# Routed experts' weight scales: one bfloat16 sum an expert earlier, five weight slots, expert 0 prepared during routing, the second token tile turned by TensorE

## The reference, cut to what matters

```
logits = x @ wg.T;  gates = softmax(logits)
w_topk, idx_topk = top_k(gates, 8);  w_topk /= sum(w_topk)
buf = zeros(64, 160, 256).at[se, rank].set(x[st], mode='drop')   # tokens of each expert
h = einsum('ech,efh->ecf', buf, expert_w1)                       # 64 x (1536 x 256)
x1, x2 = split(h, 2)
out = einsum('ecf,ehf->ech', x1 * silu(x2), expert_w2)           # 64 x (256 x 768)
combined = zeros(2048, 256).at[st].add(out[se, rank] * w)        # where rank < 160
return shared_expert(x) + combined
```

## Time and profile before

| | us |
|---|---|
| median of 3 runs | 2089.8 (2089.48 to 2091.47) |
| the profiled execution, whole | 2087.55 |
| its span, first to last instruction | 2085.5 |
| TensorE busy | 2045.9 |
| VectorE busy | 1606.5 |
| ScalarE busy | 1399.0 |
| GpSimd busy | 492.7 |
| recurrence, feed-forward and dense experts | about the first 1333 |
| routing and shared expert | about 1333 to 1459 |
| routed experts | 1459 to the end |

### The profile page before, as it was taken

How to read it: one execution, slowest core, us unless ns; L and a number is a source line. 1 busy time by engine, 2 the same in 40 slices (tenths; PEclk the granted TensorE clock), 3 DMA queues, 4 the chain that set the end, 5 groups by cost and what they waited for, 6 DMA issues and landing times. The chain is left out here.

```text
span 2085.5 us, 84981 instructions
## 1 busy us (share of the span) xinstructions
PE 2045.9 (98%) x34658; PEld 1904.1 (91%) x34658; DVE 1606.5 (77%) x8214; ACT 1399.0 (67%) x4373; POOL 492.7 (24%) x560
## 2 busy tenths in 40 slices
PE   8999999999999999999999999999899999999997
PEld 7899999999999999999867888866899999999997
DVE  7887877887787878877845555486888888888885
ACT  4665665665656655655555767643888898888894
POOL 0000000000000000000000000154677767777674
PEclk6555555555555555555599999999999999999999
DMA  4001000000000000000002233210888888888883
GB/s 130 4 4 44 4 4 4 4 4 4 4 4 4 4 4 4 4 4 4 4 1 79 93 100 104 110 61 28 312 279 302 277 296 284 296 283 303 281 301 67
DMA packets 55559, 213.85 MB, mean 103 GB/s; under 512 B 11579, under 2 KB 40961, under 8 KB 46977
## 3 DMA queue, kind: packets, MB, share of 16 engines
q1 hardware_dynamic: 36276, 184.41, 23.9%
q0 software_dynamic: 17408, 23.61, 6.0%
q10 hardware_dynamic: 1484, 0.40, 0.1%
HBM read 192.82 MB, written 15.57 MB: 100 GB/s over the span
## 5 line engine op out<-in xcount | busy, mean ns | idle before, releaser
L1987 PE MATMUL bank<-xe_part,up_part 128*128 128x160 f16 x4608 | 339.7, 233 | 3.0 <-DVE up_part L2090 3.0
L1987 PEld LDWEIGHTS bank<-xe_part,up_part 128*128 128x128 f16 x4608 | 325.9, 98 | 6.6 <-issue 3.2
L1717 POOL MEMSET cum<- 128x320 f32 x1 | 0.4, 364 | 1333.3 <-POOLq L1084 1333.3
L542 ACT ACTIVATE r_h<-bank 128x8 f32<-128x8 f32 x512 | 92.7, 181 | 276.1 <-PE bank L899 275.7
L899 PEld LDWEIGHTS bank<-keep_part,Us 128*128 128x128 f16 x6120 | 273.5, 111 | 0.4 <-issue 0.4
L2090 DVE SCALAR_TENSOR_TENSOR up_part<-ring,turn,up_part 128x1024 f16<-128x1024 f32 x192 | 246.4, 1284 | 17.4 <-ACT up_part L2036 12.2
L899 PE MATMUL bank<-keep_part,Us 128*128 128x4 f16 x6120 | 255.6, 170 | 0.0
L899 PE MATMUL bank<-raw,Us 128*128 128x4 f16 x6132 | 240.2, 167 | 0.7 <-issue 0.7
L1997 PE MATMUL bank<-mid,ring 128*128 128x160 f32 x1536 | 235.9, 303 | 1.2 <-DVE mid L2115 1.2
L1926 POOL DMA_INDIRECT out_rows<-res,to_row x128 | 213.0, 1664 | 65.5 <-issue 30.2
L2036 ACT ACTIVATE up_part<-ring,turn 128x1024 f16<-128x1024 f32 x192 | 219.5, 1144 | 0.0
(11 more groups left out here) (304 smaller groups left out, 4622.2 us busy)
## 6 DMA issues: line engine op xcount, KB each, us to landing
ring<-in_ew SPq DMA_DIRECT2D x64, 2304.0 KB
raw<-in_L_cond_ew SPq DMA_DIRECT2D x16, 1024.0 KB, 6.3
ctx_rows<-rows SPq DMA_DIRECT2D x2, 1280.0 KB, 6.7
dense_w<-in_L_ffn_W SPq DMA_DIRECT2D x2, 1024.0 KB, 9.6
dense_w<-in_L_cond_sw SPq DMA_DIRECT2D x2, 1024.0 KB, 6.5
out_rows<-res,to_row POOLq DMA_INDIRECT x128
xT<-in_xT SPq DMA_DIRECT2D x2, 864.0 KB, 10.7
dense_w<-in_sw1T SPq DMA_DIRECT2D x1, 1536.0 KB, 9.7
```

Source lines behind the costliest of these rows:

```text
L542: nc.scalar.activation(r, pre_of(0, q, jj), ACT.Tanh, scale=inv[0]).then_inc(s_r, 1)
L1987: last = nc.tensor.matmul(to[:, f * CAP:(f + 1) * CAP], w1[w][e % 2][:, i, k, s_, f * P:(f + 1) * P], xe[x][e % 2][:, k], start=(k == 0 an ...
```

## The change

The change does the following:

- The squares of expert e+3 are made in one pass over all 3072 columns (`weights_squared`), as ScalarE's last work but the down copy in expert e. TensorE sums them in expert e+1 with a bfloat16 matmul of one column (it reads the upper half of the float32 number, `coarse`), which stands after the second up group, and writes beside the down result of bank 6 or 7. VectorE's chain of four steps becomes three.
- TensorE turns the late 32 rows too (`Split.turn_tokens`), so the tokens of an expert are split by one instruction on ScalarE and one on VectorE. `turn_late` and two small VectorE instructions are gone.
- The weight ring has five slots. They lie over memory that is free by then: slot 2 over the stored rows, slot 3 over the shared expert's parts, slot 4 over the inputs. The loads of experts 2 and 3 are issued during routing, that of expert 4 once the last base rows are copied.
- Expert 0's tokens and weights are turned and split during the last down product of the shared expert, in `routing`.
- The second base turn stands between the 8th and the 9th down matmul of expert 0. The last expert's turn-out of expert 62 stands after its first up group.

The diff, cut to its core:

```diff
-RING = 4
+RING = 5
+EARLY_SCALES = 3
+def coarse(marks, at, n):
+    return marks.bitcast(BF16)[:, 2 * at + 1:2 * (at + n):2]
...
+        inputs_states = sb("inputs_and_states", [P, TALL + KD * B * S])
+        third = sb("rows_then_ring2", [P, TILES * ROW])
+        ring += [third[:, 0:WROW], sb("ring3", [P, 2 * PART])[:, 0:WROW], inputs_states[:, 0:WROW]]
...
+class Split:
+    def turn_tokens(self, to, ident, e):
+        for k in range(KD):
+            self.nc.tensor.transpose(to[:, k, 0:P], self.got[e % GOT][0][:, k * (P + NE):k * (P + NE) + P], ident[:])
+            last = self.nc.tensor.transpose(to[:, k, P:CAP], self.last_rows[e % GOT][:, k, 0:P], ident[0:CAP - P, 0:CAP - P])
+        return last
+    def low_tokens(self, low, turned, high):
+        return self.nc.vector.scalar_tensor_tensor(out=low, in0=turned, scalar=self.scale_x, in1=high, op0=ALU.mult, op1=ALU.subtract)
...
 # routing, SyncE
+                sp.wait_ge(s_rows, 96)
+                sp.dma_start(ring[2], A["ew"][2]).then_inc(s_ew[2], 16)
...
+                sp.wait_ge(s_up, 2 * B * KF)
+                sp.dma_start(ring[3], A["ew"][3]).then_inc(s_ew[3], 16)
 # routing, TensorE, in the last down product
+                            if (b, d, f) == (B - 1, 1, 1):
+                                pe.wait_ge(s_got[0], 32)
+                                pe.wait_ge(s_sc, 2)
+                                split.turn_tokens(first_tokens, ident, 0).then_inc(s_tin, 1)
 # routing, ScalarE
-                        if 1 <= b <= AHEAD and f < PAIRS:
+                        if 1 <= b <= EARLY_SCALES and f < PAIRS:
...
+                    if b == B - 1:
+                        act.wait_ge(s_wlo, KF)
+                        act.wait_ge(s_sc, 5)
+                        for i in range(PAIRS):
+                            split.high_weights(first_up[0], 0, i).then_inc(s_whi, 1)
 # experts, SyncE
-                for e in range(AHEAD, NE):
-                    if e == RING:
+                for e in range(RING - 1, NE):
+                    if e == RING - 1:
                         sp.wait_ge(s_bc, B * KD)
 # experts, TensorE
                 def sum_squares(e):
-                    pe.wait_ge(s_sq, FIRST_SQ + (e - AHEAD + 1) * PAIRS)
-                    pe.wait_ge(s_x, e * 3)
-                    nc.tensor.matmul(square_sums, ones[:], marks[:, MARK_SQ + e * PAIRS:MARK_SQ + (e + 1) * PAIRS],
-                                     start=True, stop=True).then_inc(s_ss, 1)
+                    pe.wait_ge(s_sq, FIRST_SQ + e - EARLY_SCALES + 1)
+                    pe.wait_ge(s_ye, e - 2)
+                    nc.tensor.matmul(square_sum(e), ones_bf[:], coarse(marks, MARK_SQ + e, 1), start=True, stop=True).then_inc(s_ss, 1)
...
-                turn_in(0)
                 for e in range(NE):
...
                     up(e, 0)
+                    if last_one:
+                        turn_out(e - 1)
                     up(e, 1)
-                    if e + 1 < NE:
+                    if e and e + 2 < NE:
+                        sum_squares(e + 2)
+                    if not last_one:
                         turn_in(e + 1)
                     if e == 0:
                         turn_base(0)
                     up(e, 2)
...
                     down(e, range(0, 4))
-                    if e + AHEAD < NE:
-                        sum_squares(e + AHEAD)
+                    if e == 0:
+                        turn_base(1)
                     down(e, range(4, KF)).then_inc(s_y, 1)
 # experts, ScalarE
-                    if after:
-                        weights_squared(e + AHEAD, 0)
...
-                    if after:
-                        weights_squared(e + AHEAD, 1)
                     silu(e, 2)
+                    if ahead:
+                        weights_high(e + 1, 2)
                     if e == 0:
                         store_base(1)
-                    if after:
-                        weights_squared(e + AHEAD, 2)
-                    if ahead:
-                        weights_high(e + 1, 2)
+                    if e + EARLY_SCALES < NE:
+                        weights_squared(e + EARLY_SCALES)
```

215 lines of the change are left out of this document (111 added, 104 removed).

## The result

| | before | changed |
|---|---|---|
| median, us | 2089.64 (2088.02 to 2091.47, 8 runs) | 2096.18 (2094.31 to 2096.83, 8 runs) |
| span of the profiled execution | 2085.5 | 2094.8 |
| TensorE busy | 2045.9 | 2060.9 |
| VectorE busy | 1606.5 | 1518.7 |
| ScalarE busy | 1399.0 | 1386.1 |

The ratio is 1.0031 with a 95% interval of 1.002 to 1.0042: the changed kernel is slower, by 6.5 us, where I had forecast 2070 and a range of 2059 to 2080. VectorE and ScalarE have less to do, and the time went up all the same.

What follows compares the result with a forecast made beforehand. TensorE's queue and its waits were taken as the bound, 9.45 us an expert. Gains of 12.8 - 0.2 + 6.0 + 1.1 = 19.7 us took the span from 2085.5 to 2065.8, the median to 2070 us; range 2059 to 2080.

Steps and rivals of the forecast that it cites:

- the two late transposes: TensorE, each expert: two added 32-row token transposes at 0.10 us each, 0.20 the pair, from 0.06 to 0.24.
- the entrance: From routing into the first experts: 7.7 us earlier, less 1.7 of waits, so 6.0 us gained (4.2 to 7.7).
- the sum of squares: TensorE's down product: 0.48 us go in 61 experts; a one-column matmul costing 0.07 (0.03 to 0.12) replaces them.
- ScalarE: Steady experts: one square of 2.86 us replaces three totalling 3.12; 8.5 us of work fits under 9.20, costing nothing.
- VectorE: Steady experts: four block transposes (0.93 us), two small operations and a reduction go; not the bound, so no gain.
- the ring: Five weight slots in the steady stretch: still some 16 us for each transfer, no wait on loads, so no effect.
- A: Rival: GpSimd's scatter chain keeps its old pace, 9.4 us an expert; 2081 to 2083 us; chance 0.08.
- B: Rival: DMA engines run out of pauses, scatters land in about 7.6 us, loop 10.3; 2130 us; chance 0.04.
- C: Rival: ScalarE's chain sets the period, 9.35 us an expert; 2079 us in total; chance 0.08.
- D: Rival: TensorE's moved sum matmul still waits for its squares, 9.48 us an expert; 2087 us; chance 0.03.
- the late load of expert 4: First experts: its square starts about 20 us in, wanted at 17; TensorE waits cost 1.7 us (0 to 3.5).
- the end: Last experts: expert 62's turn-out moves ahead by 3.3 us, so expert 63's scatter starts sooner; 1.1 us gained (0 to 1.6).

Runs made afterwards that it cites:

- the repeat: The changed kernel itself, unaltered, measured again beside three of its variants: 2094.46 us, ratio 1.0038 to the kernel before.
- the order of pairs: Changed kernel with the same four token transposes reordered, both 128-row ones first, then both 32-row ones: 2081.87 us, ratio 0.9967.
- the single remedies: Changed kernel with either expert 3's load held until expert 0's rows landed (2093.85 us), or expert 4's square and sum moved into expert 2 (2091.64 us).

## Why the prediction was wrong, point by point

**The term that failed: the two late transposes, 0.20 us with bounds 0.06 and 0.24.** They cost 0.62, three times as much and beyond the upper bound. The 0.42 too little are 25.6 us over 61 experts. That this is about the whole miss (26.2) is chance: the entrance missed as well, and the sum matmul, the down product and the rare stalls gave some back (the account is at the end of this section). The sum had the costs of the transposes and nothing for the step from one height to the other. I priced them by columns and by the nearest narrow matmul, the 3-column one, which is 128 rows high like its neighbours. I wrote that no row shows a 32-row load, and looked no further; but the trace of before has a tile of 4 rows among tiles of 128. TensorE, and then its weight loads:

```profile
1158.53 0.40 PE L1212 MATMUL bank<-ckd,ones 4*128 4x24 f32 x2
1158.86 1.43 PE L1160 MATMUL bank<-x_part,weights_part 128*128 128x512 f32 x5
```

```profile
1158.53 0.29 PEld L1212 LDWEIGHTS bank<-ckd,ones 4*128 4x128 f32 x2 [0.35 <-issue]
```

One float32 matmul of 24 columns (two records) takes 0.33 us, and its load, not waiting for any engine, starts after 0.35 us of standing still, together with its matmul. By that row a late transpose costs up to 0.33 and the pair up to 0.66: an expert of 9.66 us and a kernel slower than before would have been in my range. The same trace had the counterpart in every expert: the turn-out's narrow tiles of full height (L1969, "128*32") pay nothing. It is the height that counts.

The Trainium skill states the rule, in "TensorEngine Tiling (Array Packing)", section "Key Properties": changing the tiling mode, unlike changing the tile within a mode, drains TensorE. The runs agree for a change of height and give the price that it leaves open, 0.11 to 0.13 us a change here; for a change of width alone, 128 columns to 32, they show none. The section I cited instead, on the time of a weight load, was near in its figure for a load (0.107 us by it; the late tiles' loads last 0.13, those of full height in a stream follow each other by 0.11) and silent on when the load may start.

**Right, the sum of squares.** 0.48 us gone from the down product; 0.03 for the new one, 0.07 forecast. With the late rows on VectorE an expert takes 8.96 = 8.93 + 0.03.

**Right, ScalarE, VectorE and the ring** in the steady stretch: the square 2.76 us, no wait for weights, and no sign of rivals A, B, C and D. VectorE was not the bound, so taking the late rows off it could gain nothing: I said so, and that should have made any price on TensorE's side suspicious, since the move had nothing to pay for it.

**Wrong, the entrance: 6.0 us sooner forecast (4.2 to 7.7), 2.3 to 2.9 us later measured**, to the start of expert 4 (two profiles). Two steps failed. That TensorE "pays 0.4 for the four transposes inside routing" left out what it might have to wait for: the rows land beside a weight load issued in the same microsecond, TensorE waits 2.1 to 2.9 us for them, and the clock falls to its lower level behind the wait. And the late load of expert 4, which I did describe with its place and gave 1.7 us (0 to 3.5), took 12.5 us where I put 9.81. In the repeat it costs 4.0 us in expert 2, with some of it again through the clock; in the first profile 1.4 us there, behind 1.9 us that expert 1 lost by a stop without a known cause. Taking away the first wait gains 4 us at the start of expert 4 in the profiles, the second 4, both 5, measured against the repeat: they overlap. The medians show less for the first (1.0026 against 1.0031 and 1.0038, 1 to 2.5 us).

**Right in kind, the end:** 1.1 forecast with 1.6 as the most, 1.75 measured, and gone again at 8.96 us an expert.

From the forecast span of 2065.8 to the measured 2094.8 it is 29.0 us. Experts 4 to 62 took 7.1 us more than before, where the forecast has them 12.0 shorter: 19.1 (late transposes 24.8; 5.7 back, mainly from a sum matmul of 0.03 in place of 0.07, stalls that did not come, and a down product shorter by 0.03). The entrance is 9.5 (64.5 against 55.0), the work upstream 1.1 (its start differs by up to 2.6 us among the profiles), the end 0.65 back.

## What to carry to other kernels

Before a matmul or a transpose is added to TensorE's stream, compare its tile's height with that of its neighbours: each change cost 0.11 to 0.13 us here, which a price by columns or bytes doesn't contain, and here padding the tile to full height saved 0.39 of 0.60 us, putting the short ones side by side 0.26. Work that is taken off an engine that waits anyway brings nothing, so any cost at the engine that sets the pace decides. A gather that an engine will wait for should not be issued in the same microsecond as a load of megabytes; and when the load is held back, look what then stands beside it (here the next gather, for which the end of the stage waited). At a stage's entrance one ought to walk through the queue behind each late transfer, since what is moved an "expert ahead" moves its wait for data ahead too.

## What the hardware showed that I had not expected

- A change of tile height on TensorE costs 0.11 to 0.13 us, with 32 rows as with 64 (periods 9.565 and 9.62 us; 9.18 with the same tiles at full height). A 32-row transpose between its like costs 0.06 us, less than one of 128 rows (0.11). A change of width alone costs nothing that shows (0.11 us each for "128*128" and "128*32" in turn-out).
- The granted clock fell to 0.50 behind a TensorE wait of 2.1 to 2.9 us at the entrance, and made eight matmuls of 512 columns 5.1 to 6.5 us long that take 3.70 at 1.00. In expert 2, waits of 1.77, 2.13, 2.92 and 3.24 us were followed by a slow stretch, one of 2.25 us was not. The kernel before did so too: its wait of 3.03 us in expert 0 was followed by 0.50 (1472 to 1474 us), the one of 3.01 us ahead of expert 0 was not. So the length of the wait alone doesn't tell.
- Two fetches of 160 rows together landed 2.3 and 3.2 us after issue, and 8.6 us each beside a 2304 KB load.
- Entrances that differ only in the turns came out between 61.7 (four late transposes in a row) and 64.5 us (the changed kernel and the order of pairs). Two microseconds at such a place are no evidence by themselves, which is why the gains of the single remedies are read from the waits in the timelines as much as from the medians.
- A group of 24 matmuls took 2.77 us and not 1.67, in bursts with gaps of 0.17 to 0.24 us that nothing on record ended, 4 to 7 us after a weight load was issued. Its cause stays open.
